# The rotary cosine product of an attention and mixture-of-experts kernel takes its scale as a scalar

## The chip, the cores and the metric

The kernel runs on one core of one Trainium2 chip. The metric is the device time of one execution in microseconds (us). TensorE (PE) does the matrix products, VectorE (DVE), ScalarE (ACT) and GpSimd (POOL) the elementwise work, and the queue of SyncE (SP) issues most DMAs.

## What is computed

One transformer layer over 4096 tokens of width 256. The part that matters here is the front of the attention: layer norm, projection to q, k and v, rotary embedding of q and k, `elu + 1`, then causal linear attention. Cut to that, the reference is:

```
def apply_rope(x):                      # x: (B, N, H, 16), half = 8
    x1, x2 = (x[..., :half], x[..., half:])
    return concatenate([x1 * cos - x2 * sin, x1 * sin + x2 * cos], axis=-1)
x = x + attn(layernorm(x), w_qkv, w_out)
#   q, k, v = split(x @ w_qkv);  q = elu(apply_rope(q) * SCALE) + 1;  k likewise
#   out_t = q_t . cumsum(k v) / max(q_t . cumsum(k), 1e-6);  out @ w_out
x = x + ffn(layernorm(x), Wg, Wu, Wd, Wr, temperature)
#   sum over 8 experts of weight_e * (silu(x @ Wg_e) * (x @ Wu_e)) @ Wd_e
```

The division by the standard deviation of the first layer norm commutes with the projection. The kernel projects x with mean-free weights and multiplies the result by 1/std afterwards.

## The kernel before

Tokens are cut into 32 tiles of 128 (index g), four tiles into a block of 512. The attention goes tile by tile. The expert layer goes unit by unit, 16 units for each block (8 experts, two halves of the inner width), each of three products: gate, up and down. Float32 products are made of three products of rounded halves ("hi" and "lo"), so most tensors have a hi part, written by ACT, and a lo part, written by DVE or POOL.

Each engine has a program that is a hand-written list of steps. The first lists (a head, about the first 85 us) run the attention of tiles 0 to 4 while the expert weights are loaded. Then a loop over s = 5 to 35 runs, in each pass, the front of tile s (called a), the rest of tile s - 1 (called c) and four expert units (n to n + 3) of an earlier block. Every fourth pass also has the router of a block. A short tail ends with the last four units. Waits are on semaphores: `w.wait_ge(s_x, count)` ahead of an instruction.

The rotary embedding of tile g, in the order in which its steps depend on each other:

- `qkv(g)` on PE (L297, L298) writes q and k, unscaled, into a PSUM bank of 512 columns (`front`, for tiles 1 and 3 `up`), and v beside it.
- `rstd1_pow(g)` on POOL (L1134) writes 1/std, one number for each row, into `rstd1`.
- `qk_copy(g)` on ACT (L529) copies q and k into `qk` in SBUF, multiplied by 1/std.
- `sin(g, half)` on POOL (L1146), twice for each tile, multiplies that copy by the sine tables into `rop2`.
- `tcos_scale(g)` on DVE (L777) multiplies the 8 cosines of a row by 1/std into `tcos`.
- `cos(g)` on DVE (L784) multiplies the PSUM bank in place by `tcos`, repeated for 64 groups of 8 columns. It waits for `qk_copy(g)`, which reads the same bank.
- `rope(g)` on DVE (L794) adds both products into `rop`. Then come `exp(g)` on ACT (L544), `phi(g)` on DVE (L802), the hi parts on ACT (L551, L560), the lo parts on DVE (`q_lo` L810, `k_lo` L829), the transposing DMAs on SP (L1251, L1258) and `scores(g)` on PE (L320).

The table `tab` (cosine, minus sine, sine) comes to SBUF as `tabs`, one block of 512 tokens at a time, in two buffers. `load_tab` on SP waits until the block that used the buffer has been read. `rstd1` has 8 columns, and `rstd1_pow(g)` waits until the readers of tile g - 8 are done. In the loop, the list of DVE has `mean_var(a + 1); tcos_scale(a); x_lo(a + 1); acc; acc; acc; var_eps(a + 1)`, then `cos(a); h_up(n); rope(a)`. `acc` (L1056) adds an expert's output, times a scalar read from SBUF, and `x1_add` (L887) adds the attention's output to x. `x_lo(g)` (L746) makes the lo part of tile g's input, for `qkv(g)`. `h_up` (L1040) multiplies silu(gate) by up. `norm` (L872) writes the normalised attention output, which PE transposes (L365). `mask` (L819) applies the causal mask to scores.

Of the kernel before, what the change touches and what calls it, by code (L numbers as in the profile page):

```python
# [11 lines left out]
ALU = mybir.AluOpType  # L12
# [3 lines left out]
P = 128  # L16
# [53 lines left out]
def build(nc, x, xT, w_qkv, w_out, Wg, Wu, Wd, Wr, temperature, tab, out):  # L70
# [8 lines left out]
    with ctx:  # L79
# [27 lines left out]
        ve2 = sb("ve2", [P, 1])  # L107
        rstd1 = sb("rstd1", [P, NRS])
        rstd2 = sb("rstd2", [P, 1])
        tcos = sb("tcos", [P, HALF])  # L110
        qk = sb("qk", [P, 2 * D])
        rop = sb("rop", [P, 2 * D])
        rop2 = sb("rop2", [P, 2 * D])
# [35 lines left out]
            for n in ("gate", "up", "y0", "y1", "front0", "front1", "back0", "back1"))  # L149
# [29 lines left out]
             "x_hi", "qk", "v", "exp", "q_hi", "k_hi", "v1", "v2", "a_hi", "s1", "s2", "o_hi", "logit_rows_copied", "th",  # L179
             "e1", "fb", "x2_hi", "g", "h_hi"))  # L180

        (s_slab_lov, s_xlo, s_bn, s_mv, s_ve, s_tcos, s_cos, s_rope, s_phi, s_qlo, s_klo, s_amask, s_o, s_ss, s_den, s_rec, s_norm, s_olo, s_x1,
         s_bn2, s_mv2, s_ve2, s_x2n, s_x2lo, s_h, s_acc, s_hlov) = (sem(n) for n in (
             "slab_lo_v", "x_lo", "bn", "mv", "ve", "tcos", "cos", "rope", "phi", "q_lo", "k_lo", "masked", "o", "ss", "den", "rec", "norm",
             "o_lo", "x1", "bn2", "mv2", "ve2", "x2n", "x2_lo", "h", "acc", "h_lo_v"))
        ROUTE = ("sum", "inh", "off", "zone", "dist", "zone2", "m", "eq", "w0", "c", "ws", "ix", "no", "s1", "nd",
                 "m2", "fbn", "eq2", "c2", "ix2", "s2", "s12", "fw", "w", "w2", "w3", "w4", "wo")
# [49 lines left out]
        def live(g):  # L237
            return 0 <= g < NTL
# [442 lines left out]
        def vector_program(v):  # L681
# [86 lines left out]
                w.wait_ge(s_mv, g + 1)  # L768
                v.tensor_scalar(ve[:, g % NRS:g % NRS + 1], mv[:, 1:2], EPS, None, ALU.add).then_inc(s_ve, 1)

            def tcos_scale(g):
                if not live(g):
                    return
                w.wait_ge(tab_in[g // NT % 2], 16 * (g // NT // 2 + 1))
                w.wait_ge(s_cos, g)
                w.wait_ge(s_rstd1, g + 1)
                v.tensor_scalar(tcos[:, :], tabs[:, g // NT % 2, g % NT, 0:HALF], rstd1[:, g % NRS:g % NRS + 1], None, ALU.mult).then_inc(s_tcos, 1)  # L777

            def cos(g):
                if not live(g):  # L780
                    return
                w.wait_ge(s_tcos, g + 1)
                w.wait_ge(s_qkc, g + 1)
                v.tensor_tensor(qk_bank(g)[:, :].rearrange("p (h d) -> p h d", d=HALF),  # L784
                                qk_bank(g)[:, :].rearrange("p (h d) -> p h d", d=HALF), bcast(tcos[:, :], 1, 4 * H),
                                ALU.mult).then_inc(s_cos, 1)

            def rope(g):
                if not live(g):
# [273 lines left out]
            for g in range(1, NT):  # L1063
                bn(g); mean_var(g); var_eps(g)

            tcos_scale(0); wout_lo(); x_lo(1); cos(0); rope(0); phi(0); tcos_scale(1); q_lo(0); cos(1); k_lo(0)
            rope(1); x_lo(2); phi(1); tcos_scale(2); slab_lo(2); q_lo(1); mask(0, 0); mask(0, 1); k_lo(1)
            mask(0, 2); rtemp_half(); mask(0, 3); cos(2); o_sum(0, 0); bn(4); o_sum(0, 1); rope(2); den_max(0)
            tcos_scale(3); den_rec(0); mask(1, 0); phi(2); norm(0); st_add(0); mask(1, 1); x_lo(3); q_lo(2)
            mask(1, 2); k_lo(2); mean_var(4); var_eps(4); mask(1, 3); o_lo(0); slab_lo(5); cos(3); x1_add(0); bn2(0)  # L1070
            mean_var2(0); o_sum(1, 0); var_eps2(0); o_sum(1, 1); bn(5); mask(2, 0); st_add(1); den_max(1); ln2(0)
            rope(3); mask(2, 1); den_rec(1); mean_var(5); norm(1); x_lo(4); phi(3); x2_lo(0); mask(2, 2); mask(2, 3)
            q_lo(3); tcos_scale(4); o_lo(1); k_lo(3); cos(4); x1_add(1); bn2(1); mean_var2(1); var_eps2(1)
            o_sum(2, 0); o_sum(2, 1); ln2(1); den_max(2); slab_lo(8); den_rec(2); st_add(2); wr_lo(); norm(2)
            mask(3, 0); mask(3, 1); x2_lo(1); rope(4); o_lo(2); mask(3, 2); mask(3, 3); phi(4); x1_add(2); bn2(2)
            mean_var2(2); var_eps2(2); k_lo(4); q_lo(4); o_sum(3, 0); o_sum(3, 1); ln2(2); den_max(3); den_rec(3)
# [2 lines left out]
            for s in range(LAG, STEPS):  # L1079
                a, c, n = s, s - 1, NT * (s - LAG)  # L1080
                router = (s - LAG) // NT if (s - LAG) % NT == 0 else -1
                mask(c, 2); acc(n - 4, 0); bn(a + 1); slab_lo(slab(s, 0)); mask(c, 3); route_sum(router)
                mean_var(a + 1); tcos_scale(a); x_lo(a + 1); acc(n - 4, 1); acc(n - 4, 2); acc(n - 4, 3)
                var_eps(a + 1); route_zone(router); route_nearest(router); cos(a); h_up(n); rope(a); o_sum(c, 0)
                o_sum(c, 1); den_max(c); phi(a); route_weight(router); den_rec(c); slab_lo(slab(s, 1))
                route_first(router); norm(c); route_second(router); q_lo(a); k_lo(a); o_lo(c); h_up(n + 1)
                st_add(c); route_tie(router); x1_add(c); acc(n - 2, 0); bn2(c); route_ix2(router); acc(n - 2, 1)
                mean_var2(c); acc(n - 2, 2); route_s2(router); slab_lo(slab(s, 2)); var_eps2(c); acc(n - 2, 3)
                h_up(n + 2); route_both(router); ln2(c); mask(a, 0); mask(a, 1); x2_lo(c); route_out(router)
                slab_lo(slab(s, 3)); h_up(n + 3)  # L1090
# [13 lines left out]
        def gpsimd_program(pool):  # L1104
# [22 lines left out]
            def rstd1_pow(g):  # L1127
                if not live(g):
                    return
                w.wait_ge(s_mhalf, 1)  # L1130
                w.wait_ge(s_v, g - NRS + 1)
                w.wait_ge(s_tcos, g - NRS + 1)
                w.wait_ge(s_ve, g + 1)
                pool.tensor_tensor(rstd1[:, g % NRS:g % NRS + 1], ve[:, g % NRS:g % NRS + 1], mhalf[:, :], ALU.pow).then_inc(s_rstd1, 1)  # L1134

# [83 lines left out]
        def sync_program(sp):  # L1219
            w = Waits(sp)  # L1220

            def load_xr(g):
                if not live(g):
                    return
                w.wait_ge(s_xlo, g - 1)
                sp.dma_start(xr[:, g % 2, :, :], xT[:, g * P:(g + 1) * P].rearrange("(k p) n -> p k n", p=P)).then_inc(
                    xr_in[g % 2], 16)

            def load_tab(b):
                if not 0 <= b < NB:  # L1230
                    return
                w.wait_ge(s_tcos, NT * (b - 1))
                w.wait_ge(s_sin, 2 * NT * (b - 1))
                sp.dma_start(tabs[:, b % 2, :, :], tab[b * B:(b + 1) * B, :].rearrange("(t p) n -> p t n", p=P)).then_inc(
                    tab_in[b % 2], 16)

            def load_xa(g):
                if not live(g):
                    return
                if 10 <= g < 12:  # L1240
                    w.wait_ge(*slab_lo_done(SLABS - NSL))
                if g >= NXA:
                    w.wait_ge(y_out[g % 4], 16 * ((g - NXA) // 4 + 1))
                sp.dma_start(xa[:, g % NXA, :], x[g * P:(g + 1) * P, :]).then_inc(xa_in[g % 4], 16)

            def transpose_q(g):
                if not live(g):
                    return
                w.wait_ge(s_qlo, g + 1)
                w.wait_ge(s_av, 2 * (g - 1))  # L1250
                sp.dma_start_transpose(qT[:, g % 2, :, :], q_st[:, :, :, :].rearrange("p h c d -> p (h c d)")).then_inc(qT_in, 16)  # L1251

            def transpose_k(g):
                if not live(g):
                    return
                w.wait_ge(s_klo, g + 1)
                w.wait_ge(s_qk, 2 * g)
                sp.dma_start_transpose(kT[:, :, :], k_st[:, g % 2, :, :, :].rearrange("p h c d -> p (h c d)")).then_inc(kT_in, 16)  # L1258

            def store_y(g):  # L1260
                if not live(g):
                    return
                w.wait_ge(s_acc, NT * E * (g // NT + 1) - NT + g % NT + 1)
                sp.dma_start(out[g * P:(g + 1) * P, :], xa[:, g % NXA, :]).then_inc(y_out[g % 4], 16)

            def load_wqkv(k):
                sp.dma_start(wq_raw[:, k, :], w_qkv[k * P:(k + 1) * P, :]).then_inc(c_wqkv[k], 16)

            def load_small():
                sp.dma_start(wo_raw, w_out.rearrange("(k p) n -> p k n", p=P)).then_inc(c_wout, 16)  # L1270
                sp.dma_start(wr_sb[:, :, :], Wr.rearrange("(k p) n -> p k n", p=P)).then_inc(c_wr, 16)
                sp.dma_start(temp[:, :], temperature.rearrange("(a n) -> a n", a=1).broadcast_to([P, 1])).then_inc(c_temp, 16)

            load_wqkv(0); load_wqkv(1)
            load_xr(0); load_xa(0); load_xr(1)
            for g in range(1, NT):
                load_xa(g)
            load_tab(0)
            load_small()
            for s in range(STEPS):  # L1280
                load_xr(s + 2)
                transpose_q(s); transpose_k(s)
                if (s - LAG) % NT == 0:
                    for t in range(NT):
                        store_y(s - LAG - NT + t)
                if s:
                    load_xa(s + NT - 1)
                if s % NT == 0:
                    load_tab(s // NT + 1)

            for t in range(NT):
                store_y(NTL - NT + t)
            for i in range(4):
                w.wait_ge(y_out[i], 16 * NB)
# [36 lines left out]
```

## Time and profile before

| What | us |
| --- | --- |
| median of 3 runs | 805.64 |
| lowest and highest of them | 805.07 and 806.11 |
| the profiled execution | 806.51 |
| its span in the profile | 804.7 |
| PE busy | 761.0 |
| DVE busy | 603.9 |
| POOL busy | 482.7 |
| ACT busy | 465.1 |

The profile is of one execution. Its own time is 806.51 us, of which 804.7 us are the span from its first to its last instruction and 1.8 us lie around it. It is 0.9 us above the median of the three timed runs. Busy times are shares of that span. The granted clock is what the throttle left of TensorE's full speed in a stretch, in tenths on the page, as a fraction in the view by stretches.

### The profile page before, as it was taken

The page shows a single profiled execution, that of the slowest core. Times are in us where ns is not written, and L with a number is a line of the kernel's source. Part 1 is how long each engine was busy: PE and PEld are TensorE (multiplying, and loading weights), DVE is VectorE, ACT ScalarE, POOL GpSimd, SP SyncE. Part 2 cuts the span into 40 slices and gives each one's busy share as a digit, 9 for nine tenths or more (in the row PEclk, how much of TensorE's full clock was granted, in tenths as well). Part 3 has the DMA queues.
Part 4 walks back from the last instruction along what each step waited for, and adds up shares of the span by engine and source line. Part 5 has one row for each costly group of instructions (what it writes and reads, how often), then busy time and mean ns, then how long its engine had stood idle before and what let it go on. Part 6 is the DMA issues. An engine that isn't in the chain of part 4 may idle for free.

```text
span 804.7 us, 18060 instructions
## 1 busy us (share of the span) xinstructions
PE 761.0 (95%) x6660; PEld 655.0 (81%) x6660; DVE 603.9 (75%) x1597; ACT 465.1 (58%) x886; POOL 482.7 (60%) x537
## 2 busy tenths in 40 slices
PE   4475899999999999999999999999999999999998
PEld 3364688888888888888888888888888888888887
DVE  6788797878877797778877697877877788756244
ACT  3664666666666555566665566666656665634222
POOL 3685678765666666556667565565675656653322
PEclk9666799999999999999999999999999999999999
DMA  4644134122210222122111221120211121100000
GB/s 140 128 100 109 43 82 92 41 43 68 40 19 23 44 66 41 41 43 38 44 27 40 43 67 40 41 42 9 60 42 40 40 54 28 28 1 27 1 1 27
DMA packets 97320, 38.27 MB, mean 48 GB/s; under 512 B 74193, under 2 KB 96977, under 8 KB 97233
## 3 DMA queue, kind: packets, MB, share of 16 engines
q1 hardware_dynamic: 90704, 30.83, 17.8%
q10 hardware_dynamic: 6528, 6.29, 2.7%
q8 instruction: 53, 0.87, 0.4%
q14 instruction: 35, 0.28, 0.1%
HBM read 16.13 MB, written 4.19 MB: 25 GB/s over the span
## 4 chain that ended last, share of the span: by engine, by line
PE 88%; DVE 5%; POOL 2%; ACT 2%; issue 1%; DMA 1%; SPq 0%; DVEq 0%; ACTq 0%; POOLq 0%
PE gate L422 22%; PE y L455 22%; PE up L422 21%; PE front L297 5%; PE back L342 3%; PE front L298 3%; PE back L378 2%; PE back L353 2%; PE up L390 1%; PE front L320 1%; PE front L403 1%; PE back L335 1%; PE back L365 1%; POOL a_lo L1167 1%; PE back L320 1%
## 5 line engine op out<-in xcount | busy, mean ns | idle before, releaser
L1196 POOL TENSOR_TENSOR h_lo<-work,h_hi 128x512 fp32r<-128x512 f32 x126 | 163.3, 1296 | 59.7 <-ACT h_hi L657 59.7
L1167 POOL TENSOR_TENSOR a_lo<-am,a_hi 128x512 f16<-128x512 f32 x120 | 144.2, 1203 | 55.3 <-ACT a_hi L584 52.6
L455 PE MATMUL y<-wd_hi,h_hi 128*128 128x256 f32 x504 | 145.8, 289 | 0.0
L455 PE MATMUL y<-wd_lo,h_hi 128*128 128x256 f32 x504 | 141.9, 282 | 0.0
L455 PE MATMUL y<-wd_hi,h_lo 128*128 128x256 f32 x504 | 141.3, 280 | 0.0
L1040 DVE TENSOR_TENSOR work<-work,up 128x512 f32<-128x512 f32 x128 | 87.1, 680 | 70.6 <-PE up L422 70.2
L1056 DVE SCALAR_TENSOR_TENSOR xa<-y,wo,xa 128x256 f32<-128x256 f32 x252 | 111.9, 470 | 2.0 <-PE y L455 2.0
L657 ACT ACTIVATE h_hi<-work 128x512 fp32r<-128x512 f32 x126 | 79.3, 629 | 58.6 <-DVE work L1040 37.0
L455 PEld LDWEIGHTS y<-wd_lo,h_hi 128*128 128x128 f32 x504 | 94.9, 188 | 3.0
L455 PEld LDWEIGHTS y<-wd_hi,h_hi 128*128 128x128 f32 x504 | 95.0, 188 | 2.9
L584 ACT ACTIVATE a_hi<-am 128x512 f16<-128x512 f32 x120 | 74.9, 625 | 35.1 <-DVE am L819 35.0
L455 PEld LDWEIGHTS y<-wd_hi,h_lo 128*128 128x128 f32 x504 | 95.1, 189 | 0.0
L649 ACT ACTIVATE work<-gate 128x512 f32<-128x512 f32 x128 | 75.8, 592 | 30.5 <-PE gate L422 18.8
L422 PE MATMUL gate<-x_hi,wg_hi 128*128 128x512 f32 x256 | 83.3, 407 | 0.3 <-ACT work L649 0.3
L422 PE MATMUL up<-x_hi,wu_hi 128*128 128x512 f32 x256 | 81.8, 401 | 0.0
L422 PE MATMUL gate<-x_lo,wg_hi 128*128 128x512 f32 x256 | 80.8, 397 | 0.0
L422 PE MATMUL gate<-x_hi,wg_lo 128*128 128x512 f32 x256 | 80.7, 397 | 0.0
L422 PE MATMUL up<-x_hi,wu_lo 128*128 128x512 f32 x256 | 79.8, 393 | 0.0
L1155 POOL TENSOR_TENSOR vs<-vs,vx 128x256 f32<-128x256 f32 x32 | 21.7, 677 | 96.8 <-ACT vx L571 96.8
L422 PE MATMUL up<-x_lo,wu_hi 128*128 128x512 f32 x256 | 79.6, 392 | 0.0
L1146 POOL TENSOR_TENSOR rop<-qk,tabs 128x256 f32<-128x256 f32 x64 | 45.1, 725 | 35.5 <-ACT qk L529 35.4
L422 PEld LDWEIGHTS gate<-x_hi,wg_lo 128*128 128x128 f32 x256 | 48.6, 190 | 11.3
(217 smaller groups left out, 1740.2 us busy)
## 6 DMA issues: line engine op xcount, KB each, us to landing
xr<-xT SPq DMA_DIRECT2D x32, 128.0 KB, 2.4
xa<-x SPq DMA_DIRECT2D x32, 128.0 KB, 2.6
out<-xa SPq DMA_DIRECT2D x32, 128.0 KB, 1.7
xa<-Wg ACTq DMA_DIRECT2D x8, 256.0 KB, 3.0
work<-Wd ACTq DMA_DIRECT2D x8, 256.0 KB, 2.7
work<-Wu ACTq DMA_DIRECT2D x8, 256.0 KB, 2.9
work<-w_qkv SPq DMA_DIRECT2D x2, 384.0 KB, 3.8
qT<-q_st SPq DMA_TRANSPOSE x32, 3.2
```

The lines of the kernel that those rows point to most:

```text
L297: pe.matmul(qk_bank(g)[:, :], lhs, wqkv_p[wi][:, k, 0:2 * D], start=first, stop=last)
L298: m = pe.matmul(R1[:, 0:D], lhs, wqkv_p[wi][:, k, 2 * D:], start=first, stop=last)
L422: m = pe.matmul(ps, weights[wi][:, e_, k, m_ * P:(m_ + 1) * P], x2[xi][:, b % 2, k, :], start=(n == 0), stop=(n == 3 * KD - 1))
L455: m = pe.matmul(y_bank(n, t), h_at(hi, n)[:, t * P:(t + 1) * P], wd_p[wi][:, u // KI, u % KI, :], start=(n % KI == 0 and (t % 2 == 0 or n ...
L584: act.activation(a_p[0][:, heads(r), :], am_place(g, r).rearrange("p (h n) -> p h n", h=4), ACT.Copy).then_inc(s_ahi, 1)
L649: act.activation(hb[:, n % 2, :], G[:, :], ACT.Silu).then_inc(s_g, 1)
L657: act.activation(h_at(0, n), hb[:, n % 2, :], ACT.Copy).then_inc(s_hhi, 1)
L1040: v.tensor_tensor(hb[:, n % 2, :], hb[:, n % 2, :], U[:, :], ALU.mult).then_inc(s_h, 1)
L1056: v.scalar_tensor_tensor(out=xs, in0=y_bank(n, t), scalar=wo[:, b % 2, t, e_:e_ + 1], in1=xs, op0=ALU.mult, op1=ALU.add).then_inc(s_acc, 1)
L1146: pool.tensor_tensor(r2_h[:, :, half, :], qk_h[:, :, 1 - half, :], bcast(tabs[:, g // NT % 2, g % NT, at:at + HALF], 1, 2 * H), ALU.mult). ...
L1167: pool.tensor_tensor(a_p[1][:, heads(r), :], am_place(g, r).rearrange("p (h n) -> p h n", h=4), a_p[0][:, heads(r), :], ALU.subtract).then ...
L1196: pool.tensor_tensor(h_at(1, n), hb[:, n % 2, :], h_at(0, n).bitcast(F32), ALU.subtract).then_inc(s_hlo, 1)
```

## The change

The step `tcos_scale` and its buffer `tcos` are dropped. `cos(g)` becomes one scalar-tensor-tensor operation: (PSUM bank times `rstd1` of the row) times the plain cosine table of the tile, read from `tabs` with the same repetition. The calls of `tcos_scale` go out of the list of DVE. Nothing else changes its place. Two waits that counted `tcos_scale` now count `cos`: that of `rstd1_pow` and that of `load_tab`. `cos` itself now waits for the table and for 1/std.

```diff
-            def tcos_scale(g):
+            def cos(g):
                 if not live(g):
                     return
                 w.wait_ge(tab_in[g // NT % 2], 16 * (g // NT // 2 + 1))
-                w.wait_ge(s_cos, g)
                 w.wait_ge(s_rstd1, g + 1)
-                v.tensor_scalar(tcos[:, :], tabs[:, g // NT % 2, g % NT, 0:HALF], rstd1[:, g % NRS:g % NRS + 1], None, ALU.mult).then_inc(s_tcos, 1)
-
-            def cos(g):
-                if not live(g):
-                    return
-                w.wait_ge(s_tcos, g + 1)
                 w.wait_ge(s_qkc, g + 1)
-                v.tensor_tensor(qk_bank(g)[:, :].rearrange("p (h d) -> p h d", d=HALF),
-                                qk_bank(g)[:, :].rearrange("p (h d) -> p h d", d=HALF), bcast(tcos[:, :], 1, 4 * H),
-                                ALU.mult).then_inc(s_cos, 1)
+                qk_r = qk_bank(g)[:, :].rearrange("p (h d) -> p h d", d=HALF)
+                v.scalar_tensor_tensor(out=qk_r, in0=qk_r, scalar=rstd1[:, g % NRS:g % NRS + 1],
+                                       in1=bcast(tabs[:, g // NT % 2, g % NT, 0:HALF], 1, 4 * H), op0=ALU.mult,
+                                       op1=ALU.mult).then_inc(s_cos, 1)
...
-            tcos_scale(3); den_rec(0); mask(1, 0); phi(2); norm(0); st_add(0); mask(1, 1); x_lo(3); q_lo(2)
+            den_rec(0); mask(1, 0); phi(2); norm(0); st_add(0); mask(1, 1); x_lo(3); q_lo(2)
...
-                mean_var(a + 1); tcos_scale(a); x_lo(a + 1); acc(n - 4, 1); acc(n - 4, 2); acc(n - 4, 3)
+                mean_var(a + 1); x_lo(a + 1); acc(n - 4, 1); acc(n - 4, 2); acc(n - 4, 3)
...
                 w.wait_ge(s_v, g - NRS + 1)
-                w.wait_ge(s_tcos, g - NRS + 1)
+                w.wait_ge(s_cos, g - NRS + 1)
...
-                w.wait_ge(s_tcos, NT * (b - 1))
+                w.wait_ge(s_cos, NT * (b - 1))
                 w.wait_ge(s_sin, 2 * NT * (b - 1))
```

How it stands on DVE in the head, around tile 2's rotary embedding, before (`den` and `rec` are the divisor of the attention and its inverse, `nat` is the output of `norm`):

```order
L794 SCALAR_TENSOR_TENSOR rop<-front,rop 128x512
L858 TENSOR_SCALAR den<-osb 128x16
L777 TENSOR_SCALAR tcos<-tabs,rstd 128x8
L864 RECIPROCAL rec<-den 128x16
L819 TENSOR_TENSOR am<-gate,cmask 128x512
L802 SCALAR_TENSOR_TENSOR front<-front,rop 128x512
L872 SCALAR_TENSOR_TENSOR nat<-osb,rec 128x256
```

The same place on DVE after the change (its line numbers are those of the changed file):

```order
L787 SCALAR_TENSOR_TENSOR rop<-front,rop 128x512
L851 TENSOR_SCALAR den<-osb 128x16
L857 RECIPROCAL rec<-den 128x16
L812 TENSOR_TENSOR am<-gate,cmask 128x512
L795 SCALAR_TENSOR_TENSOR front<-front,rop 128x512
L865 SCALAR_TENSOR_TENSOR nat<-osb,rec 128x256
```

One row is gone, that of `tcos_scale(3)`, and what stood behind it moves up by one. All else keeps its order.

## Rows read from the trace of the kernel before

**Rows 1.** The page: busy times, granted clock in 40 slices, chain by engine

```profile
PE 761.0 (95%) x6660; PEld 655.0 (81%) x6660; DVE 603.9 (75%) x1597; ACT 465.1 (58%) x886; POOL 482.7 (60%) x537
...
PEclk9666799999999999999999999999999999999999
...
PE 88%; DVE 5%; POOL 2%; ACT 2%; issue 1%; DMA 1%; SPq 0%; DVEq 0%; ACTq 0%; POOLq 0%
```

**Rows 2.** By stretches: length, busy PE, PEld, DVE, ACT, POOL, clock, DMA, GB/s

```profile
128.00:130.00 2.00, 1.33 (x23) 1.02 (x22) 0.55 (x2) 0.25 (x1) 1.67 (x2) 1.00 0.81 238
130.00:760.00 630.00, 629.72 (x5563) 546.78 (x5563) 485.49 (x1299) 378.18 (x716) 384.55 (x421) 1.00 0.18 39
```

**Rows 3.** Waits of PE, whole span: us in total, times, longest us

```profile
PE back L365 <- DVE nat L872: 6.3, 4, 2.8
...
PE front L320 <- DMA kT<-k_st: 0.7, 1, 0.7
```

**Rows 4.** DVE groups by form: busy us, mean ns, idle before, releaser

```profile
L1056 DVE SCALAR_TENSOR_TENSOR xa<-y,wo,xa 128x256 f32<-128x256 f32 x252 | 111.9, 470 | 2.0 <-PE y L455 2.0
...
L777 DVE TENSOR_SCALAR tcos<-tabs,rstd 128x8 f32<-128x8 f32 x32 | 21.6, 676 | 0.0
L784 DVE TENSOR_TENSOR front<-front,tcos 128x512 f32<-128x512 f32 x30 | 21.0, 699 | 26.8 <-ACT qk L529 26.8
...
L887 DVE TENSOR_TENSOR xa<-back,xa 128x256 f32<-128x256 f32 x28 | 11.9, 424 | 6.0 <-PE back L378 5.6
```

**Rows 5.** Timeline of DVE in the head: start, length, instruction, idle before

```profile
37.90 0.70 DVE L777 TENSOR_SCALAR tcos<-tabs,rstd 128x8 f32<-128x8 f32 x1
38.51 0.24 DVE L864 RECIPROCAL rec<-den 128x16 f32<-128x16 f32 x1
38.67 0.62 DVE L819 TENSOR_TENSOR am<-gate,cmask 128x512 f32<-128x512 f32 x1
39.22 0.68 DVE L802 SCALAR_TENSOR_TENSOR front<-front,rop 128x512 f32<-128x512 f32 x1
```

**Rows 6.** Timeline of ACT, the same place

```profile
37.90 0.69 ACT L544 ACTIVATE front<-rop,mone 128x512 f32<-128x512 f32 x1
```

**Rows 7.** The chain that ended last, in the head: start, length, what

```profile
35.27 0.70 DVE front L784
...
47.17 0.70 DVE up L784
...
59.42 0.70 DVE front L784
```

**Rows 8.** The same chain, end of the head and first passes

```profile
84.19 2.56 PE gate L422 x6
...
98.00 2.71 PE gate L422 x6
...
102.79 1.38 PE gate L422 x6
```

**Rows 9.** Timeline of DVE in one pass of the loop

```profile
320.26 0.78 DVE L777 TENSOR_SCALAR tcos<-tabs,rstd 128x8 f32<-128x8 f32 x1
320.96 0.41 DVE L746 TENSOR_TENSOR xo_lo<-xr,xo_hi 128x256 fp32r<-128x256 f32 x1
...
323.30 0.70 DVE L784 TENSOR_TENSOR front<-front,tcos 128x512 f32<-128x512 f32 x1 [0.68 <-ACT qk L529]
...
324.88 0.69 DVE L794 SCALAR_TENSOR_TENSOR rop<-front,rop 128x512 f32<-128x512 f32 x1 [0.30 <-POOL rop L1146]
```

**Rows 10.** Timeline of POOL in the same pass

```profile
319.84 2.56 POOL L1167 TENSOR_TENSOR a_lo<-am,a_hi 128x512 f16<-128x512 f32 x2
...
323.34 0.72 POOL L1146 TENSOR_TENSOR rop<-qk,tabs 128x256 f32<-128x256 f32 x1 [0.93 <-ACT qk L529]
```

**Rows 11.** Timeline of DVE, second pass of the loop

```profile
112.11 0.90 DVE L777 TENSOR_SCALAR tcos<-tabs,rstd 128x8 f32<-128x8 f32 x1
...
115.55 0.68 DVE L784 TENSOR_TENSOR front<-front,tcos 128x512 f32<-128x512 f32 x1
...
116.92 0.69 DVE L794 SCALAR_TENSOR_TENSOR rop<-front,rop 128x512 f32<-128x512 f32 x1
```

**Rows 12.** Timeline of POOL, the same pass

```profile
115.38 1.40 POOL L1146 TENSOR_TENSOR rop<-qk,tabs 128x256 f32<-128x256 f32 x2
```

More of the change, by code:

```diff
@@ L109, in build @@
         rstd2 = sb("rstd2", [P, 1])
-        tcos = sb("tcos", [P, HALF])
         qk = sb("qk", [P, 2 * D])
@@ L180, in build @@
              "e1", "fb", "x2_hi", "g", "h_hi"))
-        (s_slab_lov, s_xlo, s_bn, s_mv, s_ve, s_tcos, s_cos, s_rope, s_phi, s_qlo, s_klo, s_amask, s_o, s_ss, s_den, s_rec, s_norm, s_olo, s_x1,
+        (s_slab_lov, s_xlo, s_bn, s_mv, s_ve, s_cos, s_rope, s_phi, s_qlo, s_klo, s_amask, s_o, s_ss, s_den, s_rec, s_norm, s_olo, s_x1,
          s_bn2, s_mv2, s_ve2, s_x2n, s_x2lo, s_h, s_acc, s_hlov) = (sem(n) for n in (
-             "slab_lo_v", "x_lo", "bn", "mv", "ve", "tcos", "cos", "rope", "phi", "q_lo", "k_lo", "masked", "o", "ss", "den", "rec", "norm",
+             "slab_lo_v", "x_lo", "bn", "mv", "ve", "cos", "rope", "phi", "q_lo", "k_lo", "masked", "o", "ss", "den", "rec", "norm",
              "o_lo", "x1", "bn2", "mv2", "ve2", "x2n", "x2_lo", "h", "acc", "h_lo_v"))
@@ L1064, in vector_program @@
                 bn(g); mean_var(g); var_eps(g)
-            tcos_scale(0); wout_lo(); x_lo(1); cos(0); rope(0); phi(0); tcos_scale(1); q_lo(0); cos(1); k_lo(0)
-            rope(1); x_lo(2); phi(1); tcos_scale(2); slab_lo(2); q_lo(1); mask(0, 0); mask(0, 1); k_lo(1)
+            wout_lo(); x_lo(1); cos(0); rope(0); phi(0); q_lo(0); cos(1); k_lo(0)
+            rope(1); x_lo(2); phi(1); slab_lo(2); q_lo(1); mask(0, 0); mask(0, 1); k_lo(1)
             mask(0, 2); rtemp_half(); mask(0, 3); cos(2); o_sum(0, 0); bn(4); o_sum(0, 1); rope(2); den_max(0)
-            tcos_scale(3); den_rec(0); mask(1, 0); phi(2); norm(0); st_add(0); mask(1, 1); x_lo(3); q_lo(2)
+            den_rec(0); mask(1, 0); phi(2); norm(0); st_add(0); mask(1, 1); x_lo(3); q_lo(2)
             mask(1, 2); k_lo(2); mean_var(4); var_eps(4); mask(1, 3); o_lo(0); slab_lo(5); cos(3); x1_add(0); bn2(0)
@@ L1072, in vector_program @@
             rope(3); mask(2, 1); den_rec(1); mean_var(5); norm(1); x_lo(4); phi(3); x2_lo(0); mask(2, 2); mask(2, 3)
-            q_lo(3); tcos_scale(4); o_lo(1); k_lo(3); cos(4); x1_add(1); bn2(1); mean_var2(1); var_eps2(1)
+            q_lo(3); o_lo(1); k_lo(3); cos(4); x1_add(1); bn2(1); mean_var2(1); var_eps2(1)
             o_sum(2, 0); o_sum(2, 1); ln2(1); den_max(2); slab_lo(8); den_rec(2); st_add(2); wr_lo(); norm(2)
```

## Prediction

> **What bounds the kernel now.** I read the busy times, the clock and the chain that ended last first. PE is busy for 761.0 of 804.7 us and makes 88% of the chain, DVE 5% [rows 1]. The view by stretches says where the rest lies: from 130 to 760 us PE is busy for 629.72 of 630 us at full clock [rows 2]. In that stretch nothing that is done on DVE can move the end, unless it makes PE wait where it does not wait now. So the change can gain only in the head, where the granted clock is 0.6 to 0.7 of full in four of the first five slices [rows 1] and PE waits for single steps of DVE, for `norm` alone 6.3 us in four waits [rows 3]. One more wait stands in the loop: 0.7 us for tile 6's transposed keys [rows 3], the hole at 128 to 130 us, where PE is busy for 1.33 of 2 us [rows 2].
>
> **What goes: 32 scalings of 8 columns.** They are busy for 21.6 us, 676 ns each on average [rows 4], as long as an operation of 512 columns, so most of this is waiting and not work. Seen by share of busy time this would be 3% of DVE. I go by place instead.
>
> In the loop, the scaling stands ahead of `x_lo` and the `acc` steps, and behind these DVE stands idle until ACT has copied q and k: 0.68 us in the pass shown, 26.8 us over 30 tiles [rows 4, 9]. `cos` starts when that copy ends, and the copy hangs on PE. A scaling that is gone makes this idle time longer and nothing earlier. Worth 0, in each of the loop's 27 tiles but the second (below).
>
> It may not even make it longer by all of its 0.78 us. The scaling ends at 321.04, inside a pair of POOL operations (319.84 to 322.40) near where the first gives way to the second, and `x_lo` behind it runs in its short 0.41 us while POOL stays busy [rows 9, 10]. That looks as if the scaling stood waiting for POOL to finish an operation. `x_lo` reads two tensors from SBUF and would then wait at that same point in its place, so the busy time of DVE should fall by less than 21.6 us, I estimate 8 to 18 us. It does not enter the sum.
>
> In the head the place that counts is tile 2. The scaling of tile 3 runs from 37.90, and the reciprocal behind it starts at 38.51, which is 0.61 us lost on DVE; mask and `phi(2)` follow without idle time, `phi(2)` at 39.22 [rows 5]. Without the scaling DVE gets to `phi(2)` at 38.61. What is late next is the exponential that it needs, which ends on ACT at 37.90 + 0.69 = 38.59 [rows 6]; with some 0.06 us from end to start `phi(2)` begins at 38.65. **Gain 0.57 us**, on the chain: from `phi(2)` it goes to `norm`, mask and the projection of tile 3, whose `cos` stands on the chain at 47.17 [rows 7]. The scalings of tiles 0, 1, 2, 4 and 5 stand where DVE then waits for a copy, a transpose or POOL anyway: 0.
>
> In the second pass of the loop the scaling (112.11, 0.90 us) has a row of operations behind it that runs without idle time up to `cos` at 115.55, so `cos` can come earlier there. But `rope` needs POOL's sine products, which end at 115.38 + 1.40 = 116.78, and it starts at 116.92 [rows 11, 12]. At most 0.14 us, less the 0.06 us from end to start: I take 0.05 us off the hole at 128 us.
>
> **What is added: a scalar read by `cos`.** The new form, a tensor in PSUM, one in SBUF and a scalar for each row, does not stand in the trace with 512 columns. With 256 it does: `acc`, 470 ns, against 424 ns for `x1_add`, the same without a scalar [rows 4]. The difference, 46 ns, is one bound. The other is 0: the scalar-tensor-tensor `rope` with an immediate takes 0.69 us for 512 columns, no more than `cos` as it is [rows 4, 9]. I take 46 ns, since `acc` is the nearer row. It counts where `cos` is on the chain of the head, for tiles 2, 3 and 4 [rows 7]: 3 x 0.046 = **0.14 us lost**. In the loop it is covered: `rope` stands idle for 0.30 us for POOL behind it [rows 9].
>
> The waits that are counted otherwise cost nothing. `rstd1_pow(g)` now waits for the `cos` eight tiles back. `load_tab` on SP stands behind the transposes of a tile whose `cos` is later than the one it waits for. The table and 1/std, for which `cos` waits now, were there for the scaling and for ACT's copy.
>
> **The sum.** In the head 0.57 - 0.14 = 0.43 us. Not all of it arrives. Towards the end of the head PE has work without a gap, at the lower clock: six products of a gate take 2.56 us at 84.19 and 1.38 us at full clock at 102.79 [rows 8]. If the clock rises when it did, PE does the work it got to earlier at half speed, and half of the lead is lost: 0.2 us is left. With 0.05 us for the hole, 0.25 us. The profiled execution would take 806.51 - 0.25 = 806.3 us; it was 0.9 us above the median, and a difference in the program holds for both, so the median goes from 805.64 to **805.4 us**. With the ends of each term (0.57 or 0.61, `cos` +0 or +0.14, all or half of the lead) it is 805.0 to 805.5; as the runs themselves spread over 1 us, 804.9 to 805.9.
>
> **A rule that speaks against it.** All 252 `acc` steps have the form of the new `cos` and average 470 ns [rows 4], which leaves no room for a half rate. The Trainium skill, page "Vector Engine (DVE) Microarchitecture Reference", section "Points that are easy to get wrong", says that a scalar-tensor-tensor whose two sources both lie in SBUF and are not bf16 runs at half rate. Here one source is in PSUM, so the trace and the page agree unless the scalar counts as a source; the first rival below has that case.
>
> **Rivals.**
> 1. *`cos` becomes slow, and the kernel slower than before.* Mechanism: the scalar and the table both come from SBUF, and the product runs at half rate. 256 columns more cost 699 - 424 = 275 ns [rows 4], so 512 columns at half rate cost 0.55 us more. On the chain of the head 3 x 0.55 - 0.57 = 1.1 us lost, half of it or all arriving, and 0.25 us for tile 5, where `rope` has 0.3 us of slack: +0.8 to +1.3 us, 806.7 us. It decides from `cos` = 0.70 + 0.57 / 3 = 0.89 us. Against it: `acc`. Chance 0.07.
> 2. *Nothing arrives.* `x_lo` or a POOL operation takes over the stall of tile 3's scaling, or the copy of the next tile is late anyway: 805.7 us, 0.12.
> 3. *The clock falls or rises at another moment.* PE's granted clock falls after idle time, the last time ahead of the gate at 98.00, which took 2.71 us in place of 1.38 [rows 8]; all PE work from 97.3 to 100.7 ran slow, 3.4 us that take 1.7 us at full clock. If a small shift keeps the clock up there, or brings the rise before 84.19 forward, the gain is 1.7 us: 803.7 us, 0.12. If a shift adds a stretch of that kind, it is 807.3 us, 0.06. The shift is only 0.4 us and the idle time of PE ahead of it hangs on steps that are not changed, so I give both little.
>
> **How the numbers follow.** Forecast 0.63, rivals 0.07, 0.12, 0.12 and 0.06. A measurement of this kernel can tell about 0.2% from no change, 1.6 us: faster means below 804.0, slower above 807.2. Below lies the good case of rival 3, with a little for a smaller one of that kind beside the forecast's lower end: 0.13. Above lies its bad case, with 0.01 for rival 1: 0.07. The rest is 0.80. The range reaches from the good case of rival 3 to the upper end of rival 1, 803.7 to 806.9 us.
>
> **What would show it.** The scaling's line is gone and DVE is busy for less, by 8 to 18 us. `cos` has a mean of 0.70 to 0.75 us, and the idle time ahead of it, for ACT, is larger than 26.8 us. PE is as busy between 130 and 760 us as before, and its stretch is as long. `phi(2)` starts 0.5 to 0.6 us earlier, the first gate 0.4 us earlier, and from 101 us on all is earlier by 0.2 to 0.4 us. The wait of 0.7 us for tile 6's keys is nearly as long. I am wrong if the slow stretches of PE's clock lie elsewhere, if `cos` is over 0.8 us, or if PE waits anew in the loop.

## The result, and the profile after

The changed kernel takes 810.34 us (median of 5 runs, 809.52 to 811.67). The kernel before, run beside it, takes 805.07 us (5 runs, 804.50 to 806.11). The ratio is 1.0057, with a 95% interval of 1.0047 to 1.0068: slower by 5.3 us, where I had forecast 805.4 us and a range that ended at 806.9. The profiled execution took 809.61 us, with a span of 807.6 us.

The page of the changed kernel (busy times, granted clock in 40 slices, chain by engine; compare rows 1):

```profile
PE 764.9 (95%) x6660; PEld 654.6 (81%) x6660; DVE 599.1 (74%) x1565; ACT 465.5 (58%) x886; POOL 481.0 (60%) x537
...
PEclk8775999999999999999999999999999999999999
...
PE 86%; DVE 5%; POOL 3%; ACT 2%; issue 1%; DMA 1%; SPq 0%; DVEq 0%; ACTq 0%; POOLq 0%
```

VectorE is busy for 4.8 us less, as it should be, and TensorE for 3.9 us more, with the same 6660 matmuls. The groups on VectorE (compare rows 4; columns as there):

```profile
L745 DVE TENSOR_TENSOR xo_lo<-xr,xo_hi 128x256 fp32r<-128x256 f32 x32 | 28.1, 879 | 0.0
L777 DVE SCALAR_TENSOR_TENSOR front<-front,rstd,tabs 128x512 f32<-128x512 f32 x30 | 22.8, 758 | 32.6 <-ACT qk L528 32.6
```

`cos` takes 758 ns, 59 more than before. `x_lo` takes 28.1 us in all and 879 ns each; before, its group was this:

```profile
L746 DVE TENSOR_TENSOR xo_lo<-xr,xo_hi 128x256 fp32r<-128x256 f32 x32 | 15.6, 487 | 0.0
```

The by-stretch view of the changed kernel (columns as in rows 2):

```profile
97.00:101.00 4.00, 3.99 (x20) 3.05 (x20) 3.84 (x10) 2.67 (x6) 2.82 (x3) 1.00 0.84 160
...
130.00:760.00 630.00, 629.64 (x5535) 543.77 (x5534) 480.16 (x1269) 375.29 (x710) 380.50 (x420) 1.00 0.18 38
```

Here the loss can be seen. In the 630 us from 130 to 760 TensorE is busy all the time and at full clock, before and after, yet it gets through 5535 matmuls where it did 5563 [rows 2]. It waits no more than before and does the same work more slowly. A stretch of ten products of 512 columns in the loop, without a wait in it, shows by how much. Timeline of TensorE before (start, length, instruction; each line is two products):

```profile
309.43 0.62 PE L422 MATMUL up<-x_hi,wu_hi 128*128 128x512 f32 x2
...
311.71 0.63 PE L422 MATMUL gate<-x_lo,wg_hi 128*128 128x512 f32 x2
```

and after, the same place:

```profile
308.06 0.62 PE L421 MATMUL up<-x_hi,wu_hi 128*128 128x512 f32 x2
...
310.38 0.63 PE L421 MATMUL gate<-x_lo,wg_hi 128*128 128x512 f32 x2
```

From the start of the first line to the start of the last it is 2.28 us before and 2.32 us after, for ten products. So that small differences can be told, I took for each trace the mean distance from one matmul's start to the next one's between 135 and 700 us, leaving out distances over 1.15 times the median, in which there is a wait. Before: gate and up 230.5 ns, down 118.1 ns. After: 233.1 and 119.3 ns. There are 1536 products of each kind in the kernel, so this makes 1536 x 2.6 + 1536 x 1.2 ns = 5.8 us. (Leaving out all over 1.05 times the median gives 230.5 and 232.8 ns for gate and up, so some tenths of a nanosecond hang on that choice.) The paces are the same early and late in the loop, and nearly so in the tail (gate and up from 760 us on, by the same rule: 231.4 and 233.5 ns), where VectorE is busy for only 17 of 48 us. That speaks against the other engines' work of the moment as the cause.

### The profile page after: what moved, and what is told of

Read it like the earlier page. It is cut to its first block, busy times and chain, and to the rows that moved or that the text cites. A ratio compares the mean times of both kernels' runs of the same rounds, so it can differ in the third digit from the quotient of the medians.

```text
span 807.6 us, 18020 instructions
## 1 busy us (share of the span) xinstructions
PE 764.9 (95%) x6660; PEld 654.6 (81%) x6660; DVE 599.1 (74%) x1565; ACT 465.5 (58%) x886; POOL 481.0 (60%) x537
## 4 chain that ended last, share of the span: by engine, by line
PE 86%; DVE 5%; POOL 3%; ACT 2%; issue 1%; DMA 1%; SPq 0%; DVEq 0%; ACTq 0%; POOLq 0%
PE y L454 21%; PE gate L421 21%; PE up L421 21%; PE front L296 5%; PE back L341 3%; PE front L297 3%; PE back L377 2%; PE back L352 2%; POOL a_lo L1160 1%; PE up L389 1%; PE front L319 1%; PE front L402 1%; PE back L334 1%; PE back L364 1%; PE back L319 1%
## 5 line engine op out<-in xcount | busy, mean ns | idle before, releaser
L421 PEld LDWEIGHTS gate<-x_lo,wg_hi 128*128 128x128 f32 x256 | 48.3, 189 | 11.8
```

What stands on the lines that cost most here:

```text
L421: m = pe.matmul(ps, weights[wi][:, e_, k, m_ * P:(m_ + 1) * P], x2[xi][:, b % 2, k, :], start=(n == 0), stop=(n == 3 * KD - 1))
```

## The experiments

```diff
         rstd2 = sb("rstd2", [P, 1])
+        hole = sb("hole", [P, HALF])
         qk = sb("qk", [P, 2 * D])
```

> The changed kernel with an unused buffer of 8 columns where tcos lay, so that all tensors behind it lie at their addresses of before. After the change the gate and up products of 512 columns follow each other on PE every 0.233 us in place of 0.230, everywhere from 102 us to the end, which makes some 5.5 us; the head is 2.6 us shorter at 126 us. Theory A (the addresses: all tensors behind tcos moved down by 32 bytes, x2 from a multiple of 64 to 32 beyond one): the pace is back at 0.230 and only the gain of the head is left, about 802.5 us. Theory B (the instruction streams: 32 instructions fewer on VectorE) and theory C (the numbers of the semaphores, one fewer): as the changed kernel, 0.233 and 810 us.

Measured: 804.63 us (before 805.59; ratio 0.9994, 0.9984 to 1.0004). Gate and up 230.4 ns, down 118.2 ns. Its by-stretch view:

```profile
130.00:760.00 630.00, 629.58 (x5564) 546.52 (x5563) 481.83 (x1271) 376.45 (x713) 381.75 (x420) 1.00 0.18 38
```

5564 matmuls, where the kernel before had 5563. An unused buffer of 32 bytes takes back all of the loss, 5.7 us. The time is not the 802.5 us that I expected, for a reason told below.

**k2_sem_kept**: the changed kernel, with an unused semaphore where `s_tcos` was.

```diff
-        (s_slab_lov, s_xlo, s_bn, s_mv, s_ve, s_cos, s_rope, ...
+        (s_slab_lov, s_xlo, s_bn, s_mv, s_ve, s_hole, s_cos, s_rope, ...
```

> The changed kernel with one unused semaphore where s_tcos was, so that all semaphores behind it have their numbers of before. Theory A (addresses) and B (instruction streams): as the changed kernel, products of 512 columns every 0.233 us, 810 us. Theory C (semaphore numbers): 0.230 us and about 802.5 us.

Measured: 810.23 us, ratio 1.0059 (1.0044 to 1.0074), 233.2 and 119.3 ns. The numbers of semaphores do nothing: theory C is out.

**k3_before_shifted**: the kernel before, with only its `tcos` allocated last.

```diff
-        tcos = sb("tcos", [P, HALF])
         qk = sb("qk", [P, 2 * D])
...
         h_p = [sb(f"h_{s}", [P, 2, B], F32R) for s in ("hi", "lo")]
+        tcos = sb("tcos", [P, HALF])
```

> The kernel before with tcos allocated last, so that all its other tensors lie where they lie in the changed kernel; nothing else differs. Theory A (addresses): the products of 512 columns come every 0.233 us and the time goes to about 810 us or more, since the head's gain is not there. Theories B and C: 0.230 us and 805.1 us, as before.

Measured: 810.72 us, ratio 1.0060 (1.0045 to 1.0075), 233.3 and 119.3 ns:

```profile
130.00:760.00 630.00, 629.77 (x5541) 544.44 (x5541) 482.16 (x1293) 376.72 (x713) 382.66 (x420) 1.00 0.18 39
```

Not one instruction is changed here, only addresses, and the whole loss is there. Theory B is out, and theory A is shown from both sides.

**k4_form_only**: `cos` in its new form, the scaling still done, its product unread. The waits of `rstd1_pow` and `load_tab` count `cos`, as in the changed kernel.

```diff
                 w.wait_ge(s_tcos, g + 1)
                 w.wait_ge(s_qkc, g + 1)
-                v.tensor_tensor(qk_bank(g)..., qk_bank(g)..., bcast(tcos[:, :], 1, 4 * H), ALU.mult).then_inc(s_cos, 1)
+                v.scalar_tensor_tensor(out=qk_r, in0=qk_r, scalar=rstd1[:, g % NRS:g % NRS + 1],
+                                       in1=bcast(tabs[:, g // NT % 2, g % NT, 0:HALF], 1, 4 * H), op0=ALU.mult,
+                                       op1=ALU.mult).then_inc(s_cos, 1)
...
-                w.wait_ge(s_tcos, g - NRS + 1)
+                w.wait_ge(s_cos, g - NRS + 1)
...
-                w.wait_ge(s_tcos, NT * (b - 1))
+                w.wait_ge(s_cos, NT * (b - 1))
```

> Half of the change: cos in its new form, and the scaling still done, its product unread; addresses, semaphores and instruction counts as before. What it tells is what the form costs: cos takes 0.76 us in place of 0.70, as in the changed kernel. Theory A, B and C alike: pace 0.230 us. The head is as before plus 3 times 0.06 us, so 805 to 805.5 us; if the head's gain of 2.6 us came from the form or the waits and not from the missing scaling, 802.5 us.

Measured: 805.11 us, ratio 0.9993 (0.9984 to 1.0003). Its groups on VectorE:

```profile
L785 DVE SCALAR_TENSOR_TENSOR front<-front,rstd,tabs 128x512 f32<-128x512 f32 x30 | 22.8, 759 | 26.2 <-ACT qk L529 26.2
L777 DVE TENSOR_SCALAR tcos<-tabs,rstd 128x8 f32<-128x8 f32 x32 | 22.1, 690 | 0.0
...
L746 DVE TENSOR_TENSOR xo_lo<-xr,xo_hi 128x256 fp32r<-128x256 f32 x32 | 15.6, 488 | 0.0
```

The slower `cos` (759 ns) costs nothing that these runs can tell from zero. And `x_lo` is short (488 ns) where the scaling stands ahead of it, and long (879 ns) where it does not: the scaling's stall passes on to `x_lo`.

### Which tensor it is

**k5_x2_only**: the changed kernel with x2 alone 32 bytes beyond a multiple of 64, all else as before within 64 bytes. x2 is the normalised input of the expert layer, the moving operand of gate and up (the one whose columns pass through TensorE); h is the stationary operand of down, and `wd`, its weights, the moving one.

```diff
+        hole = sb("hole", [P, 8])
         qk = sb("qk", [P, 2 * D])
...
+        hole2 = sb("hole2", [P, 8])
         x2 = [sb(f"x2_{s}", [P, 2, KD, B], F32R) for s in ("hi", "lo")]
+        hole3 = sb("hole3", [P, 8])
```

> The changed kernel with unused buffers so placed that x2, the moving operand of gate, up and router, lies 32 bytes beyond a multiple of 64, and every other tensor where it lay before or 64 bytes beyond. Theory A1 (a product is slow when an operand that it reads lies off a multiple of 64): gate and up come every 0.233 us, down stays at 0.118: 804.6 + 4.1 = 808.7 us. Theory A2 (other tensors, read or written by the other engines while PE reads, make the pace): 0.230 and 0.118 us, 804.6 us.

Measured: 809.49 us, ratio 1.0049 (1.0034 to 1.0064). Gate and up 233.3 ns, down 118.1 ns, as A1 said. x2 accounts for the greater part.

**k6_h_only**: the changed kernel with the addresses of before, except h, which lies where it lies in the changed kernel within 64 bytes (and within 128 at 64, where there it is at 0).

```diff
+        hole = sb("hole", [P, 8])
         qk = sb("qk", [P, 2 * D])
...
+        hole2 = sb("hole2", [P, 8])
         h_p = [sb(f"h_{s}", [P, 2, B], F32R) for s in ("hi", "lo")]
```

> The changed kernel with the addresses of before, except h, the stationary operand of down, which moves from 32 bytes beyond a multiple of 64 onto one, as in the changed kernel. Theory A1: on a multiple of 64 nothing becomes slower; down stays at 0.118 us or gains, 804.6 us or less. Theory A3 (each product depends on where its own operands lie, whatever the direction): down goes to 0.1193 us, gate and up stay at 0.230: 804.6 + 1.8 = 806.4 us. Theory A2: both stay.

Measured: 801.07 us, ratio 0.9946 (0.9930 to 0.9962): faster than either kernel. Down goes from 118.2 to 115.4 ns, gate and up to 229.7 ns:

```profile
130.00:760.00 630.00, 629.55 (x5581) 546.42 (x5580) 482.18 (x1273) 376.68 (x712) 382.32 (x420) 1.00 0.17 38
```

My label was loose: h was not moved as the change moves it, since 64 bytes turned out not to be the unit. In the changed kernel h lies at place 0 and down takes 119.3 ns; here it lies at 64 and takes 115.4.

**k7_middle_only**: the changed kernel, in which only the tensors from `qk` to `xa` are 32 bytes lower. TensorE's products for gate, up, down and qkv read none of them.

```diff
+        hole = sb("hole", [P, 8])
         x2 = [sb(f"x2_{s}", [P, 2, KD, B], F32R) for s in ("hi", "lo")]
```

> The changed kernel with x2, router, work and h where they lay before, and only the tensors from qk to xa 32 bytes lower, as in the changed kernel. Gate, up, down and qkv read none of these. Theories A1 and A3: 0.230 and 0.118 us, 804.6 us. Theory A2: gate and up at 0.233, down at 0.119, qkv at 0.1204 too, 810 us.

Measured: 804.87 us, ratio 0.9992 (0.9983 to 1.0001), 230.3 and 118.1 ns. Where the tensors that only the other engines use lie does nothing that shows here. Theory A2 is out.

**k8_64_up**: the changed kernel with everything behind `tcos`'s place 64 bytes above its address of before (a hole of 24 columns in place of 8).

```diff
+        hole = sb("hole", [P, 24])
         qk = sb("qk", [P, 2 * D])
```

> The changed kernel with every tensor behind tcos's place 64 bytes above its address of before. Theory A, if what counts is the position within 64 bytes: paces as before, 0.230 and 0.118 us, and 804.6 us. If it is the position within 128 bytes or more: another pace, up or down, and another time.

Measured: 807.89 us, ratio 1.0030 (1.0021 to 1.0040), 232.8 and 118.7 ns. The place within 64 bytes is not what counts: x2 is on a multiple of 64 as before, yet slow.

### Alone or in relation to the other operand

**k9_weights_64**: k6_h_only, with the expert weights 64 bytes higher and what lies behind them 256 bytes higher.

```diff
+        hole3 = sb("hole3", [P, 16])
         wg_p = [sb(f"wg_{s}", [P, E, KD, I], F32R) for s in ("hi", "lo")]
...
+        hole4 = sb("hole4", [P, 48])
         xr = sb("xr", [P, 2, KD, P])
```

> k6_h_only with the expert weights (the other operand of gate, up and down) 64 bytes higher and everything behind them 256 bytes higher, so that x2 and h stay at 64 beyond a multiple of 128, like the weights now. Theory R (a product is fastest when its two operands lie 64 bytes apart within 128): both pairs now lie 0 apart, so gate and up go from 0.2297 to 0.2330 us, down from 0.1154 to 0.1190, and 801 us to some 810. Theory S (only the place of x2 and h by itself counts): 0.2297 and 0.1154 us, 801 us.

Measured: 805.62 us, ratio 1.0001 (0.9991 to 1.0010). Gate and up 229.9 ns, down 119.4 ns. Each theory was right for one of the two: gate and up keep their pace, so there only x2 counts; down loses all of its gain, so there h at 64 is good only while `wd` is at 0.

**k10_xo_64**: k6_h_only, with the stationary operand of qkv 64 bytes higher.

```diff
+        hole3 = sb("hole3", [P, 16])
         xo = [sb(f"xo_{s}", [P, 2, KD, P], F32R) for s in ("hi", "lo")]
+        hole4 = sb("hole4", [P, 48])
         bst = sb("bst", [P, 6])
```

> k6_h_only with xo, the stationary operand of qkv, 64 bytes higher (from 0 to 64 within 128; its weights stay at 0 within 128) and everything behind it 256 bytes higher. Theories R and S: qkv quickens as down did, 256 columns from 0.1198 to about 0.116 us and 512 columns from 0.2318 to 0.230; 6 of each in 32 tiles make about 1 us: 800 us. Gate, up and down keep 0.2297 and 0.1154 us. Theory T (the places of x2 and h count for another reason than as operands): nothing changes, 801.1 us.

Measured: 803.40 us, ratio 0.9980 (0.9971 to 0.9989). The products of qkv with 256 columns went from 119.8 to 119.3 ns, those with 512 from 231.8 to 233.4. No gain; all three theories miss here, T the least. The time is also 2.3 us above that of k6_h_only, and down takes 116.0 ns in place of 115.4, though h and `wd` keep their places. Of the time, part can be the course of the clock in the head (see below), since k6_h_only has four runs; for the pace of down nothing here accounts.

**k11_before_h**: the kernel before, with only h 32 bytes higher.

```diff
+        hole2 = sb("hole2", [P, 8])
         h_p = [sb(f"h_{s}", [P, 2, B], F32R) for s in ("hi", "lo")]
```

> The kernel before, with nothing changed but h 32 bytes higher, as in k6_h_only. If address and instruction change simply add up: 805.7 - 3.7 = 802.0 us, down every 0.1154 us, gate and up every 0.230. The dropped scaling then accounts for the 0.9 us that k6_h_only is below.

Measured: 802.76 us, ratio 0.9967 (0.9957 to 0.9977), 229.7 and 115.8 ns. Without a changed instruction the kernel before gains 2.7 us. The rest of k6_h_only's lead, 1.7 us, is more than the 0.9 us that I gave the scaling; k6_h_only has four runs that spread over 2.3 us, so this says little on it.

**k12_weights_64_h_0**: k9_weights_64, with h 64 bytes higher.

```diff
-        hole2 = sb("hole2", [P, 8])
+        hole2 = sb("hole2", [P, 24])
         h_p = [sb(f"h_{s}", [P, 2, B], F32R) for s in ("hi", "lo")]
```

> k9_weights_64 with h 64 bytes higher: h now at 0 within 128 bytes, its partner wd at 64. Theory R for down (what counts is the distance between the two operands of down, 64 apart is fast, 0 is slow): down back from 0.1194 to 0.1155 us, 805.6 - 4.5 = 801.1 us. Theory S for down (h or wd has a good place by itself): with wd at 64 and h anywhere no better than 0.119 us, 805.6 us. Gate and up keep 0.230 us.

Measured: 802.79 us, ratio 0.9961 (0.9947 to 0.9975). Down 117.3 ns, gate and up 229.4 ns. Half of the way back: the distance between h and `wd` counts, but it is not all.

The paces together (place within 128 bytes; time from start to start, ns):

| Kernel | x2 | gate, up weights | gate and up | h | wd | down | median us |
| --- | --- | --- | --- | --- | --- | --- | --- |
| before | 64 | 0 | 230.5 | 32 | 0 | 118.1 | 805.07 |
| after | 32 | 0 | 233.1 | 0 | 0 | 119.3 | 810.34 |
| k1 | 64 | 0 | 230.4 | 32 | 0 | 118.2 | 804.63 |
| k3 | 32 | 0 | 233.3 | 0 | 0 | 119.3 | 810.72 |
| k5 | 96 | 0 | 233.3 | 96 | 0 | 118.1 | 809.49 |
| k6 | 64 | 0 | 229.7 | 64 | 0 | 115.4 | 801.07 |
| k7 | 64 | 0 | 230.3 | 32 | 0 | 118.1 | 804.87 |
| k8 | 0 | 0 | 232.8 | 96 | 0 | 118.7 | 807.89 |
| k9 | 64 | 64 | 229.9 | 64 | 64 | 119.4 | 805.62 |
| k10 | 64 | 0 | 230.0 | 64 | 0 | 116.0 | 803.40 |
| k11 | 64 | 0 | 229.7 | 64 | 0 | 115.8 | 802.76 |
| k12 | 64 | 64 | 229.4 | 0 | 64 | 117.3 | 802.79 |

## Why the prediction was wrong, point by point

**What bounds the kernel: right, and read too narrowly.** From 130 to 760 us TensorE was the bound. The step that failed is what was drawn from it: that in this stretch nothing done on VectorE can move the end unless it makes TensorE wait, with its conclusion that the change can gain only in the head. The change reached TensorE past VectorE, through the addresses: without a new wait in the stretch (TensorE is busy for 629.64 of its 630 us), gate and up went from 230.5 to 233.1 ns each. Where TensorE is busy all the time, a change of 1% in the pace of its instructions arrives in full: 5.8 us, against 0.25 us of everything that I had added up.

**A term is missing from the sum.** The buffer that goes was named in the change and given no cost, not even as a rival. None of my rivals has this mechanism. The one that ended on the slow side, `cos` at half rate, was ruled out by the trace: 758 ns, not 1.25 us.

**What goes, in the loop: right.** `cos` starts when ScalarE's copy ends, in the same idle time as before and a longer one: 32.6 us in place of 26.8. That the stall would pass on to `x_lo` was right too, and the traces bear out why: before, 29 of the 32 scalings end 26 to 33 ns after the end of a GpSimd operation; in the changed kernel 27 of the 32 `x_lo` end 278 to 286 ns after the end of one. One pass of the changed kernel (timeline of VectorE):

```profile
319.31 0.96 DVE L745 TENSOR_TENSOR xo_lo<-xr,xo_hi 128x256 fp32r<-128x256 f32 x1
...
322.40 0.76 DVE L777 SCALAR_TENSOR_TENSOR front<-front,rstd,tabs 128x512 f32<-128x512 f32 x1 [0.89 <-ACT qk L528]
```

`x_lo` takes 0.96 us where it took 0.41 [rows 9]. The Trainium skill, page "SBUF — State Buffer", section "Who interferes with whom", says that a VectorE instruction with two inputs in SBUF contends with a GpSimd instruction that reads SBUF; the trace agrees, with 487 ns before and 879 ns now that `x_lo` meets GpSimd's operation first. The amount was off: 12.5 of the 21.6 us came back on `x_lo`, 1.9 on `cos`. Added up one by one, VectorE's instructions take 7.3 us less; the page's busy time, which counts a moment once where two of them overlap, falls by 4.8 us. Both are below my 8 to 18.

**Tile 2 in the head: the size right, the next limit not.** Timeline of VectorE in the changed kernel (compare rows 5):

```profile
36.45 0.68 DVE L787 SCALAR_TENSOR_TENSOR rop<-front,rop 128x512 f32<-128x512 f32 x1
37.05 0.16 DVE L851 TENSOR_SCALAR den<-osb 128x16 f32<-128x16 f32 x1
37.24 0.25 DVE L857 RECIPROCAL rec<-den 128x16 f32<-128x16 f32 x1
37.41 0.63 DVE L812 TENSOR_TENSOR am<-gate,cmask 128x512 f32<-128x512 f32 x1
37.96 0.69 DVE L795 SCALAR_TENSOR_TENSOR front<-front,rop 128x512 f32<-128x512 f32 x1
```

The start of `rope(2)` before, ahead of what rows 5 show:

```profile
37.18 0.68 DVE L794 SCALAR_TENSOR_TENSOR rop<-front,rop 128x512 f32<-128x512 f32 x1
```

From `rope(2)` to `phi(2)` it is 1.51 us. Before, `rope(2)` started at 37.18 and `phi(2)` at 39.22, 2.04 us. That is 0.53 us less, where I had 0.57; the kernels that keep the scaling show 1.97 to 2.05 us (k3, k4, k11), the others 1.51 to 1.68. The exponential does not show as the next limit, though. `phi(2)` starts 0.55 us after the mask ahead of it in both traces, at 39.22 after 38.67 and at 37.96 after 37.41, so it follows the mask without a pause, as it did. What is lost of the 0.61 us lies before the reciprocal, which starts at 37.24 when `den_max`, whose result it needs, has just ended (37.05 + 0.16 us).

**What is added: the right row, a little low.** 59 ns for each `cos` where I took 46 from `acc`. On three of them that is 0.04 us.

**The hole at 128 us: too small a term.** I took 0.05 us for it and expected the wait for tile 6's keys to stay nearly as long as its 0.7 us. Between the first product of the fifth gate and that of the ninth, where the loop's second pass and the hole lie, TensorE is without work for 0.67 us in the kernel before, and for 0.38, 0.77 and 0.80 us in k3, k4 and k11, which keep the scaling. In the ten traces without it this is 0.00 to 0.17 us (changed kernel: 0.17). So the dropped scaling takes 0.2 to 0.8 us off this wait. My way of pricing it, through `rope` and GpSimd's sine products, allowed 0.14 us at most; by what other way it comes was not traced.

**The sum for what the edit is for.** Its test is k1_buffer_kept, the change without the shift: its median is 0.96 us below that of the kernel before, and the ratio is 0.9994 (0.9984 to 1.0004), a loss of 0.3 us to a gain of 1.3. My 0.25 us is within this, and so is no gain at all. If the sum is near, that is partly luck, since the hole gives more than I took. How much of the head's lead arrives is not shown: from trace to trace the course of the clock in the head differs by more.

**The clock in the head: a size right, a weight too low.** From the profile of the changed kernel I first read a gain of 2.6 us in the head, and built the 802.5 us of the first experiments on it. It was for the most part the clock. At 97 to 101 us the changed kernel and k1_buffer_kept show a granted clock of 1.00, the kernel before shows 0.57. That this does not come from the dropped scaling is seen in k11_before_h, which keeps the scaling and shows 1.00 as well. The kernel k2_sem_kept differs from the changed one in a semaphore's number only, and in its profiled execution it shows this:

```profile
97.00:101.00 4.00, 4.00 (x36) 3.41 (x34) 3.61 (x11) 2.56 (x6) 2.37 (x3) 0.57 0.39 74
```

That is 36 matmuls in place of 20, since other work stands there: its fifth gate starts at 109.29 us, that of the changed kernel at 106.90 and that of the kernel before at 109.21. The ten runs of k1_buffer_kept fall into 804.05 to 804.30 us (five), 804.96, and 805.85 to 806.24 us (four). The one run of them with a trace took 804.25 us and has the full clock there; that the slow group is the other course of the clock is inferred from the distance between the groups, 1.8 us, which is close to the 1.7 us at which I priced such a shift. I treated it as something that a change does or does not do. It comes and goes without an edit that bears on it, and a profile shows one course of it.

## What to carry to other kernels

Where an edit removes, adds or resizes a buffer, compare the addresses of what lies behind it, above all of TensorE's operands. If TensorE is saturated, rerun the kernel before with the addresses of after: that costs a few runs and separates what an edit does from what its shift does. When a busy engine does fewer instructions in the same busy time, look at the distance from start to start of equal instructions and not at the idle time.

## What the runs showed of the hardware

- The pace of float32 products depends on where their operands lie in a partition of SBUF; moves of 32 bytes change it, and smaller ones were not tried. With 512 columns moving it is 229.4 to 230.5 ns with x2 at place 64 and 232.8 to 233.3 ns at 0, 32 and 96 of 128 bytes. With 256 columns (down) it ranges from 115.4 to 119.4 ns: slowest with h and `wd` at the same place (119.3 and 119.4), between with 32 and 96 bytes between them (118.1 to 118.7), fastest 64 apart (115.4 to 117.3).
- The rule behind it stays open, and the place is not all that counts: with h and `wd` at the same places down took 115.4, 116.0 and 115.8 ns in k6, k10 and k11. The weights' place did not matter for gate and up, but did for down, and moving qkv's stationary operand to 64 slowed its products of 512 columns (231.8 to 233.4 ns). Whether the unit is 128 bytes or more was not separated: where x2 lay at 64 within 128, it always had the same place within 256 too.
- The bfloat16 and float16 products kept their pace in all these kernels, 25.3 ns for 51 columns of the attention, though the edits moved their operands down by 32 bytes in four of them and up by 64 in one.
- The scaling of 8 columns waited for GpSimd's operation to end, for 676 ns on average, as long as an operation of 512 columns takes. With it gone, the next step, which reads two tensors from SBUF, took over the wait (487 to 879 ns).
